# Norm, residual add and transposes between attention and FFN emitted tile by tile instead of phase by phase

## Chip, cores and metric

The kernel runs on all 8 cores of one Trainium2 chip, one batch row of 2048 tokens by 1024 features on each, with no traffic between the cores. The metric is the device time of the slowest core in microseconds (us).

## What is computed

```
x = x + layernorm(attn(layernorm(x)))
x = x + layernorm(ffn(layernorm(x)))
attn(x):  proj = layernorm(x) @ W_in -> v, g0, g1
          y = conv128(v, k0) * g0;  y = conv128(y, k1) * g1      (along the tokens)
          return x + y @ W_out
ffn(x):   s = sigmoid(x @ enc_W);  cont = s @ s2c_W;  top-2 of 8 experts on cont
          d = sigmoid(sigmoid(moe @ c2s_W) @ dec_W);  return layernorm(d)
```

All of it is float32; the experts use pairs of bf16.

## The kernel before

Each core walks through its 2048 tokens in four chunks of 512 (`q` = 0 to 3). A chunk is four tiles of 128 tokens (`t` = 0 to 3), kept in SBUF side by side as 128 partitions by 4 x 1024 columns: `s_x` (the residual stream), `s_z`, `s_xn`, `s_v`. `s_at` holds the activations transposed, features on the partitions; the matmuls read it.

The program is a list of steps. `S.add(engine, fn, reads, writes)` appends a step to the list of one engine, and a step waits by semaphore for the last writers and readers of the buffers that it names. Nothing reorders: each engine runs its steps in the order in which they were added. So the order of the Python loops is the order of the work on every engine, and a step that waits holds up all that was added behind it on the same engine.

In one chunk the stages are: the input projection (L667), two convolutions through a Fourier transform (L711, L721), the transposes of their result and the output projection (L733 to L772), the stretch that the change touches (L774 to L787), the encoder (L791, first matmul L801, weights through the two halves of `s_wb` by SyncE's DMAs), the experts, the decoder (L1046) and the final norms, which also prepare the next chunk (L1107).

The stretch of the change, with one tile at each step:

- `ln3`: `ln_steps` (L468) normalises `s_xn` tile t into `s_z` tile t. It is a chain between two engines: VectorE takes the statistics (L472, L473) and aggregates them (L475), ScalarE takes the root (L478) and negates the mean (L481), VectorE the reciprocal (L484), ScalarE makes the bias (L487) and applies scale and bias to the tile (L490, 128x1024).
- `res1` (L776): GpSimd adds `s_z` to `s_x`.
- `ln4`: `ln_steps` again, from `s_x` tile t into `s_z` tile t; it needs the sum of `res1`.
- `xfT`: `transpose_tile_to_at` (L540) transposes the eight 128x128 blocks of a tile on TensorE (L544) through the PSUM banks 4 to 7, and ScalarE copies each into `s_at` (L559). With four banks the fifth transpose waits for the first copy.

The loops are by phase. The first loop (L774) goes over the four tiles with ln3 and res1, the second (L785) over the four with ln4, and then `transpose_to_at` (L563) calls `transpose_tile_to_at` for the four tiles:

```
774        for t in range(NTQ):
775            ln_steps(xtile(s_xn, t), xtile(s_z, t), [Bxn[t]], [Bz[t]], "q%d_ln3_%d" % (q, t), slot=t)
776            S.add("gpsimd", lambda v, t=t: v.tensor_tensor(
...
785        for t in range(NTQ):
786            ln_steps(xtile(s_x, t), xtile(s_z, t), [Bx[t]], [Bz[t]], "q%d_ln4_%d" % (q, t), slot=t)
787        transpose_to_at(s_z, lambda tt: [Bz[tt]], "q%d_xfT" % q)
```

The encoder's first matmul reads block 0 of all four tiles, so it comes behind the last transposes on TensorE. The end of the chunk (L1107 to L1120) is already emitted tile by tile and has the same pattern of a norm, eight transposes and eight ScalarE evictions (L553, with scale and bias) for each tile.

Of the kernel before, what the change touches and what calls it, by code (L numbers as in the profile page):

```python
# [16 lines left out]
NTQ = TQ // CH  # L17
# [177 lines left out]
def _build(T, until="full"):  # L195
# [34 lines left out]
    def sb(name, p, cols, dt=F32):  # L230
        return nc.alloc_sbuf_tensor(name, [p, cols], dt).ap()

    s_x = sb("s_x", 128, 4096)
    s_z = sb("s_z", 128, 4096)
# [54 lines left out]
    Bx = [Buf("x%d" % t) for t in range(NTQ)]  # L289
    Bz = [Buf("z%d" % t) for t in range(NTQ)]  # L290
# [38 lines left out]
    def xtile(buf_ap, t):  # L329
        return buf_ap[:, t * D:(t + 1) * D]  # L330
# [137 lines left out]
    def ln_steps(src_ap, dst_ap, rb, wb_, tag, slot=0, extra_reads=()):  # L468
        o = slot * 16
        Bs = Bst[slot]  # L470
        st1 = S.add("vector", lambda v: (
            v.bn_stats(s_st[:, o:o + 6], src_ap[:, 0:512]),  # L472
            v.bn_stats(s_st[:, o + 6:o + 12], src_ap[:, 512:1024]))[-1],  # L473
            reads=[*rb, *extra_reads], writes=[Bs], tag=tag + "_stats")
        st2 = S.add("vector", lambda v: v.bn_aggr(s_st[:, o + 12:o + 14], s_st[:, o:o + 12]),  # L475
                    reads=[Bs], writes=[Bs], tag=tag + "_aggr")
        st3 = S.add("scalar", lambda sc: (
            sc.activation(s_st[:, o + 14:o + 15], s_st[:, o + 13:o + 14],  # L478
                          Act.Sqrt, bias=EPS),
            sc.drain(),  # L480
            sc.activation(s_st[:, o + 9:o + 10], s_st[:, o + 12:o + 13],  # L481
                          Act.Identity, bias=Z0, scale=CM1))[-1],
            reads=[Bs, Bsetup], writes=[Bs], tag=tag + "_sqrt")
        st4 = S.add("vector", lambda v: v.reciprocal(s_st[:, o + 15:o + 16], s_st[:, o + 14:o + 15]),  # L484
                    reads=[Bs], writes=[Bs], tag=tag + "_recip")
        st5 = S.add("scalar", lambda sc: (
            sc.activation(s_st[:, o + 8:o + 9], s_st[:, o + 15:o + 16],  # L487
                          Act.Identity, bias=Z0, scale=s_st[:, o + 9:o + 10]),
            sc.drain(),
            sc.activation(dst_ap, src_ap, Act.Identity,  # L490
                          bias=s_st[:, o + 8:o + 9], scale=s_st[:, o + 15:o + 16]))[-1],
            reads=[Bs, Bsetup, *rb], writes=[*wb_, Bs], tag=tag + "_apply")
        return st5
# [46 lines left out]
    def transpose_tile_to_at(tt, src_buf_ap, rbufs, tag, scale_col=None, bias_col=None):  # L540
        if True:
            for kc in range(8):
                bank = 4 + kc % 4
                S.add("tensor", lambda t, kc=kc, bank=bank, tt=tt: t.transpose(  # L544
                    pb[bank][:, tt * 128:(tt + 1) * 128],
                    src_buf_ap[:, tt * D + kc * 128: tt * D + (kc + 1) * 128],
                    IDENT),
                    reads=[*rbufs, Bsetup], writes=[Bp[bank]],
                    tag=tag + "_tp%d_%d" % (kc, tt))
                dst = s_at[:, kc * 512 + tt * 128: kc * 512 + (tt + 1) * 128]  # L550
                psl = pb[bank][:, tt * 128:(tt + 1) * 128]
                if scale_col is not None:
                    S.add("scalar", lambda sc, kc=kc, dst=dst, psl=psl: sc.activation(  # L553
                        dst, psl, Act.Identity,
                        bias=bias_col[:, kc:kc + 1], scale=scale_col[:, kc:kc + 1]),
                        reads=[Bp[bank], Bsetup], writes=[Bat[kc][tt]],
                        tag=tag + "_ev%d_%d" % (kc, tt))
                else:
                    S.add("scalar", lambda sc, dst=dst, psl=psl: sc.copy(dst, psl),  # L559
                          reads=[Bp[bank]], writes=[Bat[kc][tt]],  # L560
                          tag=tag + "_ev%d_%d" % (kc, tt))

    def transpose_to_at(src_buf_ap, rbufs_of_tile, tag, scale_col=None, bias_col=None):  # L563
        for tt in range(NTQ):
            transpose_tile_to_at(tt, src_buf_ap, rbufs_of_tile(tt), tag,
                                 scale_col=scale_col, bias_col=bias_col)
# [77 lines left out]
    for q in range(NQ):  # L644
# [22 lines left out]
        for ms in range(24):  # L667
            slot = ms % 2
# [65 lines left out]
        for ms in range(8):  # L734
            slot = ms % 2
# [38 lines left out]
        for t in range(NTQ):  # L774
            ln_steps(xtile(s_xn, t), xtile(s_z, t), [Bxn[t]], [Bz[t]], "q%d_ln3_%d" % (q, t), slot=t)
            S.add("gpsimd", lambda v, t=t: v.tensor_tensor(  # L776
                xtile(s_x, t), xtile(s_x, t), xtile(s_z, t), Alu.add),
                reads=[Bx[t], Bz[t]], writes=[Bx[t]], tag="q%d_res1_%d" % (q, t))

        if until == "attn":  # L780
            for t in range(NTQ):
                dma("sync", dy[r0 + t * 128:r0 + (t + 1) * 128, :], xtile(s_x, t),
                    reads=[Bx[t]], chan="x%d" % t, tag="q%d_xout%d" % (q, t))
            continue
        for t in range(NTQ):  # L785
            ln_steps(xtile(s_x, t), xtile(s_z, t), [Bx[t]], [Bz[t]], "q%d_ln4_%d" % (q, t), slot=t)
        transpose_to_at(s_z, lambda tt: [Bz[tt]], "q%d_xfT" % q)  # L787

        of_init = S.add("vector", lambda v: v.memset(s_of[:, :], 0.0),
                        writes=[Bof], tag="q%d_ofinit" % q)  # L790
        for g in range(4):  # L791
            for kc in range(8):
                slot = kc % 2
# [242 lines left out]
        for g2 in range(2):  # L1036
            for kc in range(16):
                slot = kc % 2
# [128 lines left out]
def build_nc(T, until="full"):  # L1167
    nc0, S0 = _build(T, until)
    with nc0.Block() as blk0:
        S0.emit(nc0, blk0, count_mode=True)  # L1170
    counts = _dma_instr_counts(nc0, S0)
    nc, S = _build(T, until)
    weights = {}
    for st0, st in zip(S0.steps, S.steps):
        if st.is_dma and st0.i in counts:
            weights[st.i] = counts[st0.i]
    with nc.Block() as blk:
        S.emit(nc, blk, dma_weights=weights)
    return nc
# [18 lines left out]
```

How the kernel before makes its waits and increments, by code:

```python
            def run(eng):  # L112
# [13 lines left out]
                            if st.chan_before > waited.get(key, 0):  # L126
                                waits[key] = max(waits.get(key, 0), st.chan_before)
                        else:
                            key = ("D", d.chan) if d.is_dma else (d.engine, False)
                            if d.target > waited.get(key, 0):
                                waits[key] = max(waits.get(key, 0), d.target)
                    if need_drain and engine_name in ("vector", "scalar", "gpsimd"):
                        eng.drain()
                        drained_upto = nloc - 1
                    for key, tgt in waits.items():
                        eng.wait_ge(sems[key], tgt)
                        waited[key] = tgt
                    inst = st.fn(eng)
                    if st.inc:
                        assert inst is not None, "step %s needs inc but returned None" % st.tag
                        inst.then_inc(sems[skey(st)], 16 if st.is_dma else 1)
                    if count_mode and st.is_dma:
                        eng.nop()
                    local_idx[id(st)] = nloc
```

## Time and profile before

| | |
|---|---|
| three runs | 3986.25, 4130.44 (median), 4306.42 us |
| profiled execution | 3991.32 us, its span 3989.7 us (core 0, the slowest of 3972.5 to 3989.7) |
| TensorE matmul | 3224.6 us busy (81%) |
| VectorE, ScalarE, GpSimd | 909.3 (23%), 796.4 (20%), 301.6 us (8%) |
| DMA | 203.79 MB, mean 51 GB/s |
| mean granted TensorE clock | 0.903 of 2.4 GHz |

A share of busy time is an average over stages. What this change is worth is read in the four stretches between the last eviction of the output projection and the first encoder matmul. A row of a timeline gives the start, the duration, the engine, the line, what is written and read, how many instructions were merged and, in brackets, how long the engine had been idle and what ended that.

### The profile page before, as it was taken

The numbers are of one execution on the slowest core, as the hardware profiler recorded it, in microseconds if no ns is written. First come the engines' busy times: TensorE is split into PE (matmuls) and PEld (weight loads), VectorE is DVE, ScalarE is ACT, GpSimd is POOL, SyncE is SP. The second block draws the span as 40 slices with busy tenths as digits, with TensorE's granted clock in tenths as the row PEclk, the third lists the DMA queues.
The fourth block names the chain that finished last, engine by engine and source line by source line (L and its number), as shares of the span: only waits on it lengthen the run. The fifth ranks groups of instructions, "written<-read, shape, count | busy, mean of one in ns | idle before, by whom it ended". The sixth has DMA issues, their size and how long they took to land.

```text
span 3989.7 us, 39388 instructions; the slowest of 8 cores (3972.5 to 3989.7 us)
## 1 busy us (share of the span) xinstructions
PE 3224.6 (81%) x14240; PEld 1862.2 (47%) x14240; DVE 909.3 (23%) x1576; ACT 796.4 (20%) x1537; POOL 301.6 (8%) x255
## 2 busy tenths in 40 slices
PE   0698997879769987978939999797975999797893
PEld 0596463323359536322419846432335953632241
DVE  0102531051110452023020153105101045202401
ACT  0300002162230002045050000216223000213502
POOL 1141000000020000000030000000002000000002
PEclk9898998998879998998969999899887999899896
DMA  3252011221123001121212200122122310112121
GB/s 63 52 136 66 0 31 43 64 53 40 66 69 84 24 0 42 61 60 32 71 64 80 66 0 25 44 70 53 37 69 64 83 30 0 42 55 60 38 64 39
DMA packets 241244, 203.79 MB, mean 51 GB/s; under 512 B 45496, under 2 KB 192968, under 8 KB 241056
## 3 DMA queue, kind: packets, MB, share of 16 engines
q1 hardware_dynamic: 231552, 174.10, 15.3%
q0 software_dynamic: 9504, 27.18, 2.8%
q8 instruction: 118, 1.93, 0.2%
q14 instruction: 70, 0.57, 0.0%
HBM read 186.02 MB, written 14.68 MB: 50 GB/s over the span
## 4 chain that ended last, share of the span: by engine, by line
PE 69%; ACT 10%; DMA 6%; DVE 5%; issue 4%; ACTq 3%; POOL 1%; POOLq 1%; DVEq 1%; SPq 0%
PE pb L683 14%; PE pb L1046 11%; PE pb L801 10%; PE pb L750 6%; PE pb L590 3%; PE pb L589 3%; PE pb L592 3%; PE pb L591 3%; PE pb L1026 3%; DMA s_big<-L_ffn_We 2%; DVE s_hl L899 2%; PE pb L625 2%; PE pb L816 2%; PE pb L544 2%; PE pb L626 2%
## 5 line engine op out<-in xcount | busy, mean ns | idle before, releaser
L683 PE MATMUL pb<-s_wb,s_at 128*128 128x128 f32 x6144 | 697.3, 277 | 60.1 <-DMA s_wb<-L_attn_W_in 34.3
L683 PEld LDWEIGHTS pb<-s_wb,s_at 128*128 128x128 f32 x6144 | 696.5, 194 | 61.2 <-issue 61.2
L1046 PE MATMUL pb<-s_big,s_wb 128*128 128x512 f32 x1024 | 451.5, 602 | 18.0 <-ACT s_xn L1056 12.2
L801 PE MATMUL pb<-s_at,s_wb 128*128 128x512 f32 x1024 | 452.7, 598 | 7.1 <-DMA s_wb<-L_ffn_enc_W 6.3
L1046 PEld LDWEIGHTS pb<-s_big,s_wb 128*128 128x128 f32 x1024 | 196.4, 193 | 276.0 <-issue 275.7
L559 ACT COPY s_at<-pb 128x128 f32<-128x128 f32 x256 | 52.4, 270 | 1321.5 <-PE pb L544 1320.0
L801 PEld LDWEIGHTS pb<-s_at,s_wb 128*128 128x128 f32 x1024 | 187.1, 190 | 269.3 <-issue 269.0
L750 PE MATMUL pb<-s_wb,s_at 128*128 128x128 f32 x2048 | 229.6, 275 | 0.0
L750 PEld LDWEIGHTS pb<-s_wb,s_at 128*128 128x128 f32 x2048 | 229.0, 192 | 0.6 <-issue 0.5
L899 DVE TENSOR_TENSOR s_hl<-s_wtmp,s_hh 128x512 bf16<-128x512 f32 x256 | 176.8, 692 | 224.5 <-ACT s_hh L896 186.7
L893 ACT ACTIVATE s_wtmp<-pb,s_be 128x512 f32<-128x512 f32 x256 | 175.7, 686 | 134.5 <-PE pb L884 112.1
L544 PE MATMUL pb<-s_cons,s_xn 128*128 128x128 f32 x128 | 42.0, 438 | 165.1 <-ACT s_xn L535 149.8
L896 ACT CAST s_hh<-s_wtmp 128x512 bf16<-128x512 f32 x256 | 158.6, 619 | 17.0 <-issue 1.0
L776 POOL TENSOR_TENSOR s_x<-s_x,s_z 128x1024 f32<-128x1024 f32 x16 | 37.5, 2346 | 1579.0 <-ACT s_z L490 1579.0
L909 PE MATMUL pb<-s_hh,s_we2h 128*64 128x512 bf16 x256 | 103.7, 405 | 64.1 <-ACT s_hh L896 58.4
L1087 DVE COPY s_z<-pb 128x128 f32<-128x128 f32 x64 | 14.1, 282 | 618.8 <-PE pb L1076 599.9
L704 DVE TENSOR_TENSOR s_big<-pb,s_bias 128x512 f32<-128x512 f32 x64 | 44.2, 691 | 441.0 <-PE pb L683 402.4
L827 DVE CAST s_conth<-s_cont 64x512 bf16<-64x512 f32 x4 | 1.7, 418 | 578.7 <-ACT s_cont L822 578.7
L917 PE MATMUL pb<-s_hl,s_we2h 128*64 128x512 bf16 x256 | 101.0, 395 | 40.1 <-DVE s_hl L899 39.8
L1026 PE MATMUL pb<-s_of,s_wb 64*128 64x512 f32 x128 | 111.9, 1065 | 10.5 <-DVE s_of L945 8.5
L625 PE MATMUL pb<-s_wtmp,s_cons 128*128 128x512 f32 x128 | 73.8, 661 | 52.7 <-DVE s_wtmp L620 52.6
L811 ACT ACTIVATE s_big<-pb,s_encb 128x512 f32<-128x512 f32 x64 | 38.8, 690 | 376.2 <-PE pb L801 376.2
(193 smaller groups left out, 3152.4 us busy)
## 6 DMA issues: line engine op xcount, KB each, us to landing
s_wb<-L_attn_W_in SPq DMA_DIRECT2D x96, 512.0 KB, 3.9
s_wb<-L_ffn_enc_W SPq DMA_DIRECT2D x128, 256.0 KB, 3.1
s_wb<-L_ffn_dec_W SPq DMA_DIRECT2D x128, 256.0 KB, 2.6
s_wb<-L_attn_W_out SPq DMA_DIRECT2D x32, 512.0 KB, 4.2
s_we1h<-we1hd SPq DMA_DIRECT2D x32, 256.0 KB, 2.7
s_we1l<-we1ld POOLq DMA_DIRECT2D x32, 256.0 KB, 3.0
y<-s_x SPq DMA_DIRECT2D x16, 512.0 KB, 2.7
s_bias<-L_attn_b_in SPq DMA_DIRECT2D x96, 64.0 KB, 4.1
```

The source lines that it names most:

```text
L544: S.add("tensor", lambda t, kc=kc, bank=bank, tt=tt: t.transpose(pb[bank][:, tt * 128:(tt + 1) * 128], src_buf_ap[:, tt * D + kc * 128: tt ...
L589: last = t.matmul(pb[bank][:, :], FWD_HI(s_i, 0), prevh, start=True, stop=False)
L590: last = t.matmul(pb[bank][:, :], FWD_HI(s_i, 1), curh, start=False, stop=False)
L625: t.matmul(pb[binv][:, :], G_HI(0), w0, start=True, stop=False)
L683: last = t.matmul(pb[bank][:, tt * 128:(tt + 1) * 128], s_at[:, kc * 512 + tt * 128: kc * 512 + (tt + 1) * 128], wap[:, kc * 128:(kc + 1) ...
L750: last = t.matmul(pb[bank][:, tt * 128:(tt + 1) * 128], s_at[:, kc * 512 + tt * 128: kc * 512 + (tt + 1) * 128], wap[:, kc * 128:(kc + 1) ...
L801: last = t.matmul(pb[mi][:, :], eap[:, mi * 128:(mi + 1) * 128], s_at[:, kc * 512:(kc + 1) * 512], start=(kc == 0), stop=(kc == 7))
L893: sc.activation(t32, pb[bank][:, :], Act.Relu, bias=s_be1[:, e * 8 + mc:e * 8 + mc + 1])
L896: return sc.copy(s_hh[:, hb * 512:(hb + 1) * 512], t32)
L899: S.add("vector", lambda v, hb=hb, t32=t32: v.tensor_tensor(s_hl[:, hb * 512:(hb + 1) * 512], t32, s_hh[:, hb * 512:(hb + 1) * 512], Alu.s ...
L1026: S.add("tensor", lambda t, mc=mc, bank=bank, half=half: t.matmul(pb[bank][:, :], s_wb[0:64, half * 1024 + (mc % 8) * 128: half * 1024 + ( ...
L1046: last = t.matmul(pb[mi][:, :], dap[:, mi * 128:(mi + 1) * 128], s_big[:, kc * 512:(kc + 1) * 512], start=(kc == 0), stop=(kc == 15))
```

## The change

The second norm and the transposes move into the loop over the tiles. Tile t now goes through ln3, res1, ln4 and its eight transposes before tile t+1 begins. The steps and their number stay as they are; `until` is "full" here.

```diff
@@ -776,15 +776,16 @@
             S.add("gpsimd", lambda v, t=t: v.tensor_tensor(
                 xtile(s_x, t), xtile(s_x, t), xtile(s_z, t), Alu.add),
                 reads=[Bx[t], Bz[t]], writes=[Bx[t]], tag="q%d_res1_%d" % (q, t))
+            if until != "attn":
+                ln_steps(xtile(s_x, t), xtile(s_z, t), [Bx[t]], [Bz[t]],
+                         "q%d_ln4_%d" % (q, t), slot=t)
+                transpose_tile_to_at(t, s_z, [Bz[t]], "q%d_xfT" % q)
...
-        for t in range(NTQ):
-            ln_steps(xtile(s_x, t), xtile(s_z, t), [Bx[t]], [Bz[t]], "q%d_ln4_%d" % (q, t), slot=t)
-        transpose_to_at(s_z, lambda tt: [Bz[tt]], "q%d_xfT" % q)
```

ScalarE, chunk 0, before: from the last instruction of ln3 of tile 0 over ln3 of tile 1, and then the end of ln4 of tile 3 and the copies (`sem_vector` is a wait for VectorE, `sem_tensor` one for TensorE, `sem_gpsimd` one for GpSimd).

```order
L490 ACTIVATE s_z<-s_xn,s_st 128x1024
L478 ACTIVATE s_st<-s_st 128x1 [waits sem_vector_False]
L481 ACTIVATE s_st<-s_st 128x1
L487 ACTIVATE s_st<-s_st 128x1 [waits sem_vector_False]
L490 ACTIVATE s_z<-s_xn,s_st 128x1024
...
L490 ACTIVATE s_z<-s_x,s_st 128x1024
L559 COPY s_at<-pb 128x128 [waits sem_tensor_False] x32
```

The next norm behind tile 0's ln3 is ln3 of tile 1, and all 32 copies stand in one piece behind the eight norms.

ScalarE, chunk 0, in the changed kernel, from the same instruction on.

```order
L490 ACTIVATE s_z<-s_xn,s_st 128x1024
L478 ACTIVATE s_st<-s_st 128x1 [waits sem_vector_False]
L481 ACTIVATE s_st<-s_st 128x1
L487 ACTIVATE s_st<-s_st 128x1 [waits sem_vector_False,sem_gpsimd_False]
L490 ACTIVATE s_z<-s_x,s_st 128x1024
L559 COPY s_at<-pb 128x128 [waits sem_tensor_False] x8
L478 ACTIVATE s_st<-s_st 128x1 [waits sem_vector_False]
```

Behind the norm of `s_xn` (ln3, tile 0) there now stands the norm of `s_x` (ln4) of the same tile, then its eight copies, and only then ln3 of tile 1.

VectorE, chunk 0, before: ln3 of tile 0 and what follows it.

```order
L472 BN_STATS s_st<-s_xn 128x6
L473 BN_STATS s_st<-s_xn 128x6
L475 BN_AGGR s_st<-s_st 128x2
L484 RECIPROCAL s_st<-s_st 128x1 [waits sem_scalar_False]
L472 BN_STATS s_st<-s_xn 128x6
```

Tile 1's statistics of `s_xn` follow without a wait.

VectorE, chunk 0, in the changed kernel, from the aggregation of ln3 of tile 0 on.

```order
L475 BN_AGGR s_st<-s_st 128x2
L484 RECIPROCAL s_st<-s_st 128x1 [waits sem_scalar_False]
L472 BN_STATS s_st<-s_x 128x6 [waits sem_gpsimd_False,sem_scalar_False]
L473 BN_STATS s_st<-s_x 128x6
L475 BN_AGGR s_st<-s_st 128x2
L484 RECIPROCAL s_st<-s_st 128x1 [waits sem_scalar_False]
L472 BN_STATS s_st<-s_xn 128x6
```

The statistics of `s_x`, which wait for GpSimd's addition, moved in front of the statistics of `s_xn` of tile 1, and those stand behind the whole ln4 of tile 0.

## Rows read from the trace of the kernel before

**Rows 1.** The page, part 4: the chain that ended last, by engine.

```profile
PE 69%; ACT 10%; DMA 6%; DVE 5%; issue 4%; ACTq 3%; POOL 1%; POOLq 1%; DVEq 1%; SPq 0%
```

**Rows 2.** Windows, chunk 0: us, busy of PE, PEld, DVE, ACT, POOL, clock, DMA, GB/s.

```profile
612.00:628.00 16.00, 0.00 (x0) 0.00 (x0) 9.69 (x24) 11.30 (x21) 9.38 (x4) 0.53 0.04 15
628.00:636.00 8.00, 1.09 (x4) 0.72 (x4) 3.84 (x10) 6.34 (x12) 0.00 (x0) 0.50 0.00 1
636.00:643.00 7.00, 6.45 (x29) 4.86 (x30) 0.00 (x0) 6.68 (x33) 0.00 (x0) 0.70 0.01 2
```

**Rows 3.** Timeline, chunk 0: ln3 and res1 of tile 0.

```profile
612.43 0.69 DVE L472 BATCH_NORM_STATS2 s_st<-s_xn 128x6 f32<-128x512 f32 x1
614.11 0.30 ACT L478 ACTIVATE s_st<-s_st 128x1 f32<-128x1 f32 x1 [60.39 <-DVE s_st L475]
615.68 1.24 ACT L490 ACTIVATE s_z<-s_xn,s_st 128x1024 f32<-128x1024 f32 x1
616.83 0.28 ACT L478 ACTIVATE s_st<-s_st 128x1 f32<-128x1 f32 x1
617.13 2.34 POOL L776 TENSOR_TENSOR s_x<-s_x,s_z 128x1024 f32<-128x1024 f32 x1 [285.20 <-ACT s_z L490]
```

**Rows 4.** Timeline, chunk 0: ln4, transposes, copies and the first encoder matmuls.

```profile
626.57 1.24 ACT L490 ACTIVATE s_z<-s_x,s_st 128x1024 f32<-128x1024 f32 x1
628.07 1.09 PE L544 MATMUL pb<-s_cons,s_z 128*128 128x128 f32 x4 [17.36 <-ACT s_z L490]
630.64 0.28 ACT L478 ACTIVATE s_st<-s_st 128x1 f32<-128x1 f32 x1
632.25 1.24 ACT L490 ACTIVATE s_z<-s_x,s_st 128x1024 f32<-128x1024 f32 x1
636.16 0.75 ACT L559 COPY s_at<-pb 128x128 f32<-128x128 f32 x4
636.55 6.32 PE L544 MATMUL pb<-s_cons,s_z 128*128 128x128 f32 x28 [7.39 <-ACT s_at L559]
637.08 6.14 ACT L559 COPY s_at<-pb 128x128 f32<-128x128 f32 x28 [0.18 <-PE pb L544]
642.70 2.80 PE L801 MATMUL pb<-s_at,s_wb 128*128 128x512 f32 x6
```

**Rows 5.** Timeline, chunk 3: first statistics of ln3, first encoder matmuls.

```profile
3468.94 0.69 DVE L472 BATCH_NORM_STATS2 s_st<-s_xn 128x6 f32<-128x512 f32 x1
3499.68 7.09 PE L801 MATMUL pb<-s_at,s_wb 128*128 128x512 f32 x16
```

**Rows 6.** Timeline, end of chunk 0, where the work already goes tile by tile.

```profile
1087.95 2.65 PE L544 MATMUL pb<-s_cons,s_xn 128*128 128x128 f32 x8 [12.43 <-ACT s_xn L535]
1088.50 2.92 ACT L553 ACTIVATE s_at<-pb,s_bA,s_gA 128x128 f32<-128x128 f32 x8 [0.69 <-PE pb L544]
1091.27 0.33 ACT L478 ACTIVATE s_st<-s_st 128x1 f32<-128x1 f32 x1
...
1099.52 2.34 POOL L1115 TENSOR_TENSOR s_v<-s_v,s_gb 128x1024 f32<-128x1024 f32 x1 [0.15 <-issue]
1101.97 0.69 DVE L472 BATCH_NORM_STATS2 s_st<-s_v 128x6 f32<-128x512 f32 x1 [3.45 <-POOL s_v L1115]
```

**Rows 7.** Windows of TensorE alone, chunk 0: us, busy us, clock, DMA share, GB/s.

```profile
636.50:639.50 3.00, 2.95 (x13) 0.50 0.00 0
639.50:640.50 1.00, 1.00 (x6) 0.67 0.00 0
640.50:642.50 2.00, 2.00 (x11) 1.00 0.03 8
```

**Rows 8.** Timeline: the first decoder matmuls of chunk 0.

```profile
946.39 14.01 PE L1046 MATMUL pb<-s_big,s_wb 128*128 128x512 f32 x27 [0.93 <-ACT s_big L1031]
```

**Rows 9.** Timeline of ScalarE, chunk 0: the copies ahead of ln3, and a table load.

```profile
547.49 6.24 ACT L559 COPY s_at<-pb 128x128 f32<-128x128 f32 x31 [0.87 <-PE pb L544]
...
671.50 1.28 ACT L811 ACT_TABLE_LOAD   x1 [28.27 <-PE pb L801]
```

## The prediction

> **What bounds the kernel now.** I read the chain that ended last first. TensorE carries 69% of it [rows 1], so any stretch in which TensorE stands still is paid in full. Then I cut chunk 0 into windows around the edited loops [rows 2]. From 612 to 628 TensorE does nothing, from 628 to 636 it has 1.09 us of work, and from 636 to 643 it runs the transposes. In the same 31 us ScalarE is busy 11.30 + 6.34 + 6.68 = 24.3 us, more than any other engine. So the stretch is bounded by ScalarE with its short chains to VectorE, and its length goes one for one into the time.
>
> The length before: from the first statistics of ln3 to the first encoder matmul it is 642.70 - 612.43 = 30.27 us in chunk 0 [rows 3, 4] and 3499.68 - 3468.94 = 30.74 us in chunk 3 [rows 5]. I take 30.5 us for each of the four chunks, 122 us in all, 3% of the time.
>
> Why it is as short as that: ln3 of tile 0 takes its root at 614.11, and ln3 of tile 1 at 616.83 [rows 3]. So eight norms pass at some 2.7 us each, since the statistics of the next tile and GpSimd's addition (617.13 to 619.47) lie beside ScalarE's work on another tile. The transposes come last, where the copies set the pace: 28 in 6.14 us [rows 4], 0.22 us each.
>
> **The change, part by part.** No instruction is added or removed, and no DMA. What moves is the order on three engines, and with it three things lose their cover.
>
> 1. The addition. VectorE now has ln4's statistics of tile t directly behind ln3's reciprocal, and they wait for GpSimd. ScalarE has ln4's root next, so it stands as well. Queued behind this wait on VectorE are ln3's statistics of tile t+1, on ScalarE the whole of ln3 of tile t+1, and TensorE waits for both. The whole 2.34 us now stands on the path, four times in a chunk.
> 2. The statistics of ln4, which follow the addition: uncovered too. Those of ln3 for tile t+1 stay covered, by ScalarE's apply and copies of tile t.
> 3. The copies. Before, the four transposes that PSUM has room for were ready when the copies began. Now each tile waits for its first transpose, and ScalarE can't start the next norm until the eighth copy.
>
> One tile in the new order, from ln3's root to the root of the next tile's ln3:
>
> - root to end of apply, ln3: 616.92 - 614.11 = 2.81 us [rows 3];
> - to GpSimd's start: 617.13 - 616.92 = 0.21 us, and its addition: 2.34 us [rows 3];
> - to VectorE's start behind GpSimd: 1101.97 - 1101.86 = 0.11 us [rows 6], where VectorE really waits for GpSimd;
> - statistics to root: 614.11 - 612.43 = 1.68 us [rows 3];
> - root to end of apply, ln4: 633.49 - 630.64 = 2.85 us [rows 4];
> - to the first transpose: 628.07 - 627.81 = 0.26 us [rows 4];
> - first transpose to first copy: 1088.50 - 1087.95 = 0.55 us [rows 6], then seven more copies at 0.22 us and 0.27 us for the last: 2.34 us together;
> - the next root overlaps the end of the last copy: -0.10 us (-0.15 in rows 6).
>
> The sum is 12.50 us a tile. A chunk is then 1.68 us for the first statistics, four tiles, 0.10 us given back at the end, less 0.52 us because the encoder starts before the last copy ends (643.22 against 642.70 [rows 4]): 1.68 + 50.00 + 0.10 - 0.52 = 51.3 us. Against 30.5 us that is 20.8 us more in a chunk, 83 us in four.
>
> The copies are the one term that the trace doesn't show in this form. From below: when transposes are ready, four copies take 0.75 us [rows 4], 0.16 us apart, which gives 1.9 us for the piece instead of 2.34. From above: the evictions of the tile-by-tile stage take 2.92 us for eight [rows 6], 3.5 us with the first transpose, but they carry a scale and a bias. I take 0.22 us, because those 28 rows are this same copy, bound by the same four banks.
>
> 4. The clock. Before, the encoder starts behind 28 transposes, at clock 1.00. The clock is 0.50 from 636.5 to 639.5, 0.67 in the next microsecond and 1.00 from 640.5 on [rows 7], and the encoder starts at 642.70. Now only eight transposes, some 1.8 us, stand between a wait of 10 us and the encoder, so its first matmuls run at 1.2 GHz. A start that is cold from the first matmul shows what it costs: the decoder's first 27 matmuls take 14.01 us [rows 8], against 0.59 + 26 x 0.44 = 12.0 us at the encoder's pace at full clock (six in 2.80 us [rows 4]). So 2.0 us is the most that I put for a chunk. If the clock comes back as long behind the first transpose as it did before (some 3.5 us), 1.7 us of the encoder pass at half pace, which loses 0.9 us. The low end is 0.4 us. I take 1.0 us, 4 us in all.
>
> The Trainium skill bears on this term. Its page "TensorE: Matmul & The Clock Gate", section "Part 4: PE-mode transpose", says that transposes don't count as work that lifts the clock. This trace disagrees: from 636.5 to 642.5 TensorE ran nothing but transposes, and the clock rose from 0.50 to 1.00 [rows 7]. By the page the encoder would start wholly cold and pay the 2.0 us, 4 us more over the run; by the row it pays about 1.
>
> Total: 83 + 4 = 87 us. The profiled execution took 3991.3 us, so the forecast is 4078 us, +2.2%. That is made against this execution. It stands at the low end of the three runs shown (3986 to 4306, median 4130), and the ratio, 1.022, is what I would carry to another level. About 2% (80 us) is what a measurement of this kernel can tell from no change.
>
> **What else could move.** The encoder's weights: two slots are filled during the stretch before and after, so their transfers stay covered. Later stages see nothing but a shift.
>
> **Rivals.**
>
> A. The same mechanism, but smaller, ending within 2%. With copies 0.16 us apart and 0.4 us for the clock, a tile is 12.07 us and a chunk 49.5 us: 4 x (19.0 + 0.4) = 78 us, 4069 us, +1.9%. For it: four copies did run at that spacing. Against it: there the transposes had been waiting for 8 us; here each copy is released by a transpose at half clock, and the fifth by a bank.
>
> B. The work hides itself after all, and the time is not slower. ScalarE would have to fill GpSimd's and VectorE's time with another tile. The place is the wait of ln4's root. If all of it were covered, a tile would cost two norms of 2.72 us and eight copies of 0.22 us, 7.2 us, and a chunk some 30 us: 3990 us, no change. The point from which it decides is 7.3 us a tile: above that the new order loses. What speaks for it is that the tail of uncovered copies shrinks from 7 us to 2.3. Against it stands that ScalarE and VectorE both run in program order, and that in the tile-by-tile stage VectorE's statistics sat idle 3.45 us behind GpSimd [rows 6].
>
> C. Something more on the path. If ScalarE had to load a table between copies and root, at 16 places and 1.28 us each, which is what the load ahead of the encoder's sigmoid takes [rows 9], it would be 20 us more, 4098 us. Or the copies go at the pace of rows 6, 1.1 us more a tile, 18 us in all, and the clock costs 2.0 us a chunk: 4100 us. Against the load: copies ended at 553.73 [rows 9] and the root at 614.11 started on VectorE's release [rows 3], with nothing in between.
>
> **How the numbers follow.** The forecast has 0.65; it ends above 2% by a small margin. A has 0.20, B 0.05 and C 0.10. The bounds of the unknown costs are 4069 and 4100; executions of one kernel differ by a few tenths of a per cent, some 12 us, which gives 4055 to 4112. Faster by over 2%: only if B went beyond full cover, 0.01. Within 2%: A and B, 0.24. Slower by over 2%: the forecast and C, 0.75.
>
> **What would show it.** In the changed trace the roots of ln3 of two neighbouring tiles stand 12.5 us apart. VectorE's statistics of `s_x` show some 4.5 us of idle time ahead of them, released by GpSimd, 16 times. TensorE's transposes come as four groups of eight with some 10 us between them. The first encoder matmul comes 51 us behind the first statistics, and the granted clock is 0.50 there, with 1.00 one to two microseconds later. The rest of each chunk keeps its length. It would be wrong if neighbouring roots were under 11 us apart (copies or addition covered), or if the encoder or a later stage changed its length by more than a microsecond or two.

## The result and the profile after

The changed kernel takes 4083.32 us in the median of ten runs, the kernel before 4001.91 us. The ratio is 1.0218, with a 95% interval of 1.0199 to 1.0237. The forecast was 4078 us and a ratio of 1.022. Some executions are slowed by a lower granted clock on one half of the chip or both (the profiled ones of the changed kernel and of e9 on cores 4 to 7), so every ratio is one of the others alone, and all rows of the changed kernel are from core 3. This ratio is that of the means 4082.2 and 3995.1 us. The span of core 3 is 4067.0 us, against 3978.5 us before: 88.5 us more.

The forecast was made against an execution of 3991 us, at the low end of the three runs that were shown then. Their median, 4130 us, isn't the level to set 4078 us against (it would make a gain of the loss that was forecast): seven more runs brought it to 4002.

The timeline of the changed kernel, core 3, chunk 0, from the first statistics of ln3 to the root of tile 1's ln3. It answers to [rows 3], and the brackets are the idle time before an instruction and what ended it:

```profile
611.38 0.69 DVE L472 BATCH_NORM_STATS2 s_st<-s_xn 128x6 f32<-128x512 f32 x1
613.07 0.29 ACT L478 ACTIVATE s_st<-s_st 128x1 f32<-128x1 f32 x1 [60.39 <-DVE s_st L475]
614.63 1.24 ACT L490 ACTIVATE s_z<-s_xn,s_st 128x1024 f32<-128x1024 f32 x1
616.08 2.33 POOL L776 TENSOR_TENSOR s_x<-s_x,s_z 128x1024 f32<-128x1024 f32 x1 [286.51 <-ACT s_z L490]
618.59 0.69 DVE L472 BATCH_NORM_STATS2 s_st<-s_x 128x6 f32<-128x512 f32 x1 [4.51 <-POOL s_x L776]
620.27 0.29 ACT L478 ACTIVATE s_st<-s_st 128x1 f32<-128x1 f32 x1 [4.40 <-DVE s_st L475]
621.89 1.24 ACT L490 ACTIVATE s_z<-s_x,s_st 128x1024 f32<-128x1024 f32 x1
623.41 2.04 PE L544 MATMUL pb<-s_cons,s_z 128*128 128x128 f32 x8 [13.75 <-ACT s_z L490]
623.95 1.86 ACT L559 COPY s_at<-pb 128x128 f32<-128x128 f32 x8 [0.82 <-PE pb L544]
625.70 0.30 ACT L478 ACTIVATE s_st<-s_st 128x1 f32<-128x1 f32 x1
```

One reads the new path down the column: GpSimd's addition ends at 618.41, and VectorE, idle for 4.51 us, starts at 618.59. ScalarE ends its apply at 615.87 and then stands for 4.40 us. In these 4.40 us no compute engine ran anything but the addition and, behind it, the statistics of `s_x` with their aggregation. From root to root a tile takes 625.70 - 613.07 = 12.63 us.

The last tile of the chunk and the encoder, same core; it answers to [rows 4]:

```profile
660.09 1.24 ACT L490 ACTIVATE s_z<-s_x,s_st 128x1024 f32<-128x1024 f32 x1
661.47 2.04 PE L544 MATMUL pb<-s_cons,s_z 128*128 128x128 f32 x8 [10.75 <-ACT s_z L490]
662.01 1.85 ACT L559 COPY s_at<-pb 128x128 f32<-128x128 f32 x8 [0.68 <-PE pb L544]
663.30 29.30 PE L802 MATMUL pb<-s_at,s_wb 128*128 128x512 f32 x64
```

The stretch is 663.30 - 611.38 = 51.92 us. The encoder's first 64 instructions take 29.30 us. (Each float32 matmul of the code shows as two instructions; 64 of them are the encoder's first group of 32.) The same instructions before, on core 3:

```profile
641.74 27.69 PE L801 MATMUL pb<-s_at,s_wb 128*128 128x512 f32 x64
```

And the clock at the encoder's start, in windows of the changed kernel, core 3 (width; busy time of TensorE, its weight loads, VectorE, ScalarE and GpSimd with instruction counts; granted clock; DMA share; GB/s):

```profile
661.00:662.00 1.00, 0.53 (x3) 0.56 (x4) 0.00 (x0) 0.33 (x1) 0.00 (x0) 0.50 0.00 0
662.00:663.00 1.00, 1.00 (x6) 0.70 (x4) 0.00 (x0) 0.95 (x5) 0.00 (x0) 0.50 0.00 0
663.00:664.00 1.00, 1.00 (x4) 0.63 (x3) 0.00 (x0) 0.86 (x4) 0.00 (x0) 0.50 0.00 0
664.00:665.00 1.00, 1.00 (x2) 0.34 (x1) 0.00 (x0) 0.00 (x0) 0.00 (x0) 0.50 0.00 0
665.00:666.00 1.00, 1.00 (x3) 0.46 (x2) 0.00 (x0) 0.00 (x0) 0.00 (x0) 0.50 0.00 0
666.00:667.00 1.00, 1.00 (x3) 0.41 (x2) 0.00 (x0) 0.00 (x0) 0.00 (x0) 0.68 0.00 0
667.00:668.00 1.00, 1.00 (x4) 0.40 (x3) 0.00 (x0) 0.00 (x0) 0.00 (x0) 1.00 0.00 0
```

```profile
663.30:666.60 3.30, 3.30 (x5) 0.50 0.00 0
1638.67:1642.80 4.13, 4.13 (x6) 0.50 0.00 0
2608.83:2612.20 3.37, 3.37 (x5) 0.50 0.00 0
3580.82:3584.90 4.08, 4.08 (x6) 0.50 0.00 0
```

All four chunks of core 3, as differences of such start times ("encoder" is from its first matmul to the table load of its first sigmoid):

| us | stretch, chunks 0 to 3 | sum | encoder, sum |
|---|---|---|---|
| before | 30.24, 30.31, 30.34, 30.61 | 121.5 | 111.3 |
| after | 51.92, 51.13, 51.71, 51.33 | 206.1 | 119.2 |
| difference | | +84.6 | +7.9 |

The rest of core 3's span is 4.0 us shorter. That says nothing of the change: within the profiled execution of the kernel before, the same rest differs by 15 us from core to core (3737.7 to 3752.5 us).

### The profile page after: what moved, and what is told of

The parts are those of the page before. It is cut to its first block, busy times and chain, and to the rows that moved or that the text cites. A ratio compares the mean times of both kernels' runs of the same rounds, so it can differ in the third digit from the quotient of the medians.

```text
span 4183.6 us, 39380 instructions; the slowest of 8 cores (4059.8 to 4183.6 us)
## 1 busy us (share of the span) xinstructions
PE 3348.2 (80%) x14240; PEld 1919.5 (46%) x14240; DVE 910.9 (22%) x1576; ACT 798.0 (19%) x1537; POOL 301.4 (7%) x255
## 4 chain that ended last, share of the span: by engine, by line
PE 70%; ACT 10%; DMA 5%; DVE 5%; issue 4%; ACTq 2%; POOL 2%; POOLq 1%; DVEq 1%; SPq 0%
PE pb L683 14%; PE pb L1047 11%; PE pb L802 11%; PE pb L750 6%; PE pb L590 3%; PE pb L589 3%; PE pb L592 3%; PE pb L591 3%; PE pb L1027 3%; DMA s_big<-L_ffn_We 2%; PE pb L625 2%; PE pb L626 2%; PE pb L817 1%; PE pb L627 1%; DVE s_hl L900 1%
## 5 line engine op out<-in xcount | busy, mean ns | idle before, releaser
L683 PE MATMUL pb<-s_wb,s_at 128*128 128x128 f32 x6144 | 699.5, 278 | 63.2 <-DMA s_wb<-L_attn_W_in 37.5
L683 PEld LDWEIGHTS pb<-s_wb,s_at 128*128 128x128 f32 x6144 | 698.3, 195 | 64.6 <-issue 64.6
L1047 PE MATMUL pb<-s_big,s_wb 128*128 128x512 f32 x1024 | 484.5, 638 | 18.9 <-ACT s_xn L1057 12.2
L802 PE MATMUL pb<-s_at,s_wb 128*128 128x512 f32 x1024 | 477.7, 628 | 3.6 <-DMA s_wb<-L_ffn_enc_W 3.4
L1047 PEld LDWEIGHTS pb<-s_big,s_wb 128*128 128x128 f32 x1024 | 207.1, 204 | 299.1 <-issue 298.0
L802 PEld LDWEIGHTS pb<-s_at,s_wb 128*128 128x128 f32 x1024 | 202.5, 201 | 275.6 <-issue 275.0
L750 PE MATMUL pb<-s_wb,s_at 128*128 128x128 f32 x2048 | 240.8, 283 | 0.0
L750 PEld LDWEIGHTS pb<-s_wb,s_at 128*128 128x128 f32 x2048 | 240.1, 200 | 0.5 <-issue 0.3
L544 PE MATMUL pb<-s_cons,s_z 128*128 128x128 f32 x128 | 32.6, 427 | 181.1 <-ACT s_z L490 181.1
```

Source lines behind the costliest of these rows:

```text
L683: last = t.matmul(pb[bank][:, tt * 128:(tt + 1) * 128], s_at[:, kc * 512 + tt * 128: kc * 512 + (tt + 1) * 128], wap[:, kc * 128:(kc + 1) ...
L750: last = t.matmul(pb[bank][:, tt * 128:(tt + 1) * 128], s_at[:, kc * 512 + tt * 128: kc * 512 + (tt + 1) * 128], wap[:, kc * 128:(kc + 1) ...
L802: last = t.matmul(pb[mi][:, :], eap[:, mi * 128:(mi + 1) * 128], s_at[:, kc * 512:(kc + 1) * 512], start=(kc == 0), stop=(kc == 7))
L1047: last = t.matmul(pb[mi][:, :], dap[:, mi * 128:(mi + 1) * 128], s_big[:, kc * 512:(kc + 1) * 512], start=(kc == 0), stop=(kc == 15))
```

## The experiments

The table has the ratio to the kernel before, run beside each, and the two sums of core 3 as above. e1 to e4 shared one set of runs of the kernel before, e5 to e7 another, e8 and e9 a third. The ratios of e5 and e8 rest on two and four runs.

| | what | ratio, 95% interval | stretch | encoder |
|---|---|---|---|---|
| after | the change | 1.0218 (1.0199 to 1.0237) | 206.1 | 119.2 |
| e1 | ln4 in the loop only | 1.0183 (1.0165 to 1.0202) | 193.6 | 111.3 |
| e2 | transposes in a loop only | 1.0054 (1.0038 to 1.0070) | 134.7 | 116.6 |
| e3 | the change, one tile of skew | 1.0067 (1.0048 to 1.0086) | 141.1 | 118.6 |
| e4 | the change, addition on VectorE | 1.0160 (1.0133 to 1.0187) | 184.1 | 116.2 |
| e5 | the change, 14 extra matmuls | 1.0235 (1.0188 to 1.0282) | 214.8 | 111.1 |
| e8 | the change, 10 extra matmuls | 1.0229 (1.0173 to 1.0285) | 204.6 | 111.4 |
| e6 | order before, gathered copies | 0.9986 (0.9976 to 0.9996) | 104.2 | 116.3 |
| e7 | e6, many extra matmuls | 0.9993 (0.9980 to 1.0007) | 114.3 | 112.1 |
| e9 | e6, few extra matmuls | 0.9950 (0.9928 to 0.9972) | 103.2 | 112.1 |

### One half of the change at a time

e1 takes the transposes out of the loop again:

```diff
             if until != "attn":
                 ln_steps(xtile(s_x, t), xtile(s_z, t), [Bx[t]], [Bz[t]],
                          "q%d_ln4_%d" % (q, t), slot=t)
-                transpose_tile_to_at(t, s_z, [Bz[t]], "q%d_xfT" % q)
...
+        transpose_to_at(s_z, lambda tt: [Bz[tt]], "q%d_xfT" % q)
```

> Only half of the change: ln4 stands behind res1 in the loop over the tiles, the 32 transposes stay behind all norms. My theory: the cost is the cover that GpSimd's addition and ln4's statistics lose. A tile is then the 12.63 us of the changed trace less its copies and first transpose, 9.9 us (2.81 + 0.21 + 2.34 + 0.11 + 1.68 + 2.85 - 0.10). Four of them, 1.68 us of statistics and the old tail of copies (7.0 us, less 0.5) give 47.8 us for the stretch against 30.5 us: +17 us a chunk, +69 us in all, and no cost in the encoder, which again starts behind 28 dense transposes. Rival: the cost comes with the transposes and copies between the norms; then this kernel stays within 20 us of the kernel before.

e2 starts from the kernel before and puts only the transposes into the loop of ln4:

```diff
         for t in range(NTQ):
             ln_steps(xtile(s_x, t), xtile(s_z, t), [Bx[t]], [Bz[t]], "q%d_ln4_%d" % (q, t), slot=t)
-        transpose_to_at(s_z, lambda tt: [Bz[tt]], "q%d_xfT" % q)
+            transpose_tile_to_at(t, s_z, [Bz[t]], "q%d_xfT" % q)
```

> Only the other half: all ln3 and res1 first, then for each tile ln4 and its eight transposes with their copies. My theory: the addition keeps its cover, and what is added is that each tile waits for its first transpose and that no copies run while ScalarE waits for nothing: 12.5 us up to ln4's first root, then 2.85 + 0.28 + 0.54 + 1.86 - 0.16 = 5.4 us a tile, 33.6 us for the stretch, +3 us a chunk. The encoder starts behind one group of eight transposes: between 0 and 2 us a chunk at half clock. Together +12 to +20 us. Rival (the transposes between the norms carry the cost): +70 us or more.

Measured, e1 adds 72.1 us to the stretch and nothing to the encoder, 1.0183 in all, where 69 us were expected. e2 adds 13.2 us to the stretch and 5.3 us to the encoder, 1.0054 in all (some 21 us, where 12 to 20 were expected). So the halves give 85.3 and 5.4 us together, and the whole change 84.6 and 7.9: in the stretch they add up, in the encoder not quite, and four fifths of the cost stand in e1, with the addition. The rival that put it on the transposes falls. The timeline of e1, core 3, one tile from ln3's root to the next, with the same wait as in the changed kernel:

```profile
612.06 0.29 ACT L478 ACTIVATE s_st<-s_st 128x1 f32<-128x1 f32 x1 [60.41 <-DVE s_st L475]
615.08 2.33 POOL L776 TENSOR_TENSOR s_x<-s_x,s_z 128x1024 f32<-128x1024 f32 x1 [285.94 <-ACT s_z L490]
617.58 0.69 DVE L472 BATCH_NORM_STATS2 s_st<-s_x 128x6 f32<-128x512 f32 x1 [4.50 <-POOL s_x L776]
619.26 0.29 ACT L478 ACTIVATE s_st<-s_st 128x1 f32<-128x1 f32 x1 [4.39 <-DVE s_st L475]
622.03 0.28 ACT L478 ACTIVATE s_st<-s_st 128x1 f32<-128x1 f32 x1
```

9.97 us a tile, where the sum said 9.90. In e2 the norms wait for no addition, and a tile of ln4 with its transposes takes 5.3 us:

```profile
635.72 0.30 ACT L478 ACTIVATE s_st<-s_st 128x1 f32<-128x1 f32 x1
638.73 2.04 PE L544 MATMUL pb<-s_cons,s_z 128*128 128x128 f32 x8 [3.26 <-ACT s_z L490]
639.27 1.85 ACT L559 COPY s_at<-pb 128x128 f32<-128x128 f32 x8 [0.68 <-PE pb L544]
641.02 0.30 ACT L478 ACTIVATE s_st<-s_st 128x1 f32<-128x1 f32 x1
```

Most of e2's 3.3 us a chunk in the stretch is one wait: ScalarE idles 0.68 us or more in each tile for the first transpose, at least 2.7 us a chunk, where before the first four copies found their transposes ready [rows 4].

### The cover given back by a skew

e3 stays tile by tile, but ln3 of tile t+1 goes ahead of ln4 of tile t:

```diff
             if until != "attn":
-                ln_steps(xtile(s_x, t), xtile(s_z, t), [Bx[t]], [Bz[t]],
-                         "q%d_ln4_%d" % (q, t), slot=t)
-                transpose_tile_to_at(t, s_z, [Bz[t]], "q%d_xfT" % q)
+                for u in ([t - 1] if t else []) + ([t] if t == NTQ - 1 else []):
+                    ln_steps(xtile(s_x, u), xtile(s_z, u), [Bx[u]], [Bz[u]],
+                             "q%d_ln4_%d" % (q, u), slot=u)
+                    transpose_tile_to_at(u, s_z, [Bz[u]], "q%d_xfT" % q)
```

> The changed kernel with one tile of skew: ln3 and res1 of tile t+1 stand ahead of ln4 and the transposes of tile t; the work is still tile by tile. My theory: what costs is only that nothing covers the addition, so the skew gives that back: 1.68 + 4 x 2.75 + 4 x 2.85 + 4 x 2.5 - 0.4 = 33.7 us for the stretch, +3 us a chunk, and 2 us a chunk for the clock in the encoder as in the changed kernel: +20 us against the kernel before, where the change costs 88. Rival (alternating between two norms and copies is what costs, by short waits at every handover): more than half of the 88 us stays.

The ratio is 1.0067: of the change's 2.2% one and a half come back. That leaves some 27 us, where 20 were expected (the two sums give 19.6 and 7.3 us). The stretch is 35.3 us a chunk where 33.7 were expected. The missing 1.6 us stand at one place, in the first tile, where one norm isn't enough to cover the addition (ScalarE idles there 1.2 to 1.6 us in the four chunks). Timeline of e3, core 3:

```profile
617.62 2.34 POOL L776 TENSOR_TENSOR s_x<-s_x,s_z 128x1024 f32<-128x1024 f32 x1 [287.48 <-ACT s_z L490]
620.06 0.69 DVE L472 BATCH_NORM_STATS2 s_st<-s_x 128x6 f32<-128x512 f32 x1 [1.74 <-POOL s_x L776]
621.74 0.29 ACT L478 ACTIVATE s_st<-s_st 128x1 f32<-128x1 f32 x1 [1.64 <-DVE s_st L475]
```

For the later tiles the eight copies of the tile before lie between as well, and ScalarE's wait is gone. So the rival (alternating norms and copies is what costs) falls; what costs is a chain with nothing of another tile in its gaps.

### The addition made shorter

e4 is the changed kernel with `res1` added to VectorE's list:

```diff
-            S.add("gpsimd", lambda v, t=t: v.tensor_tensor(
+            S.add("vector", lambda v, t=t: v.tensor_tensor(
                 xtile(s_x, t), xtile(s_x, t), xtile(s_z, t), Alu.add),
```

> The changed kernel with res1's addition on VectorE instead of GpSimd. My theory: the addition stands on the path 16 times. A 128x1024 addition on VectorE should take about 1.3 us (two 128x512 ones take 0.69 each) and start some 0.1 us behind the apply, against 0.21 + 2.34 + 0.17 us now: 1.2 us less a tile, 19 us less than the changed kernel, +69 us against the kernel before. Rival: the addition lies beside something else that is as long; then nothing changes, +88 us.

The stretch is 22.0 us shorter than in the changed kernel, 1.4 us for each of the 16 tiles; 1.2 were expected. Timeline of e4, core 3:

```profile
610.05 1.24 ACT L490 ACTIVATE s_z<-s_xn,s_st 128x1024 f32<-128x1024 f32 x1
611.39 1.23 DVE L776 TENSOR_TENSOR s_x<-s_x,s_z 128x1024 f32<-128x1024 f32 x1 [1.89 <-ACT s_z L490]
612.71 0.69 DVE L472 BATCH_NORM_STATS2 s_st<-s_x 128x6 f32<-128x512 f32 x1
```

From the end of the apply to the statistics it takes 1.42 us here and 2.72 us in the changed kernel: 1.30 us less, and the stretch is 1.38 us a tile shorter. What was taken off the addition came off the stretch in full, which is what being on the path means, and the rival (it lies beside something as long) falls. The whole time agrees, 1.0160 where 69 us make 1.017. The encoder is 3.0 us shorter too, which wasn't expected: the clock rises 2.2 to 2.7 us behind its start here.

### The clock at the encoder's start

e5 gives TensorE something to do while it waits for the last tile:

```diff
                 transpose_tile_to_at(t, s_z, [Bz[t]], "q%d_xfT" % q)
+                if t == NTQ - 2:
+                    def warm_fn(te):
+                        last = None
+                        for _ in range(14):
+                            last = te.matmul(pb[3][:, :], IDENT, s_cons[:, 0:512],
+                                             start=True, stop=True)
+                        return last
+                    S.add("tensor", warm_fn, reads=[Bsetup], writes=[Bp[3]],
+                          tag="q%d_warm" % q)
```

> The changed kernel with 14 extra 128x512 matmuls on TensorE (into PSUM bank 3, which is free then) between the transposes of tile 2 and those of tile 3, where TensorE waits 10.5 us for the last norms. They compute nothing that is used. My theory: what the change costs in the encoder (its first 64 matmuls take 29.4 to 30.1 us instead of 27.8) is the clock alone, granted at 0.50 for the first 3 us. If the extra matmuls lift it and it falls again only after a while, the encoder runs at full clock: 8 us less in all, and the stretch itself as long as before (51.5 us). If the clock has fallen again by the time the transposes come (they end some 2.5 us before the last transposes start), nothing changes. Rival: the encoder is slower by its DMAs or by PSUM; then 8 us stay while the clock is 1.00.

e5 was mis-sized: 28 instructions for 14 matmuls held the last transposes back by 2.6 us a chunk. But it answered its question: the encoder takes 111.1 us in four chunks, as before the change. e8 has 10 in place of 14.

> The kernel e5 with 10 extra matmuls in place of 14. In e5 each of them ran as two passes, so 28 passes took 13.3 us and held tile 3's transposes back by 2.6 us a chunk, while the encoder's first 64 matmuls were back at 27.8 us. With 20 passes they should end some 0.7 us ahead of the transposes. My theory: the stretch is that of the changed kernel or a little less (51.5 us, the transposes run faster), the encoder's 64 take 27.8 us: 8 us less than the changed kernel, +80 us against the kernel before. Rival: the clock falls in the gap, then +88 us.

In e8 the stretch is 204.6 us and the encoder 111.4 us: 9.3 us less together than in the changed kernel. Core 3 of e8, the timeline of chunk 0 and two windows (columns as above):

```profile
651.94 10.04 PE L787 MATMUL pb<-s_cons 128*128 128x512 f32 x20
662.90 0.63 PE L544 MATMUL pb<-s_cons,s_z 128*128 128x128 f32 x4 [0.92 <-ACT s_z L490]
664.35 27.69 PE L811 MATMUL pb<-s_at,s_wb 128*128 128x512 f32 x64
```

```profile
662.00:664.35 2.35, 1.28 (x9) 1.01 (x9) 0.00 (x0) 1.78 (x7) 0.00 (x0) 1.00 0.00 0
664.35:666.00 1.65, 1.65 (x5) 0.82 (x5) 0.00 (x0) 0.52 (x4) 0.00 (x0) 1.00 0.00 0
```

The clock stays at 1.00 over the gap of 0.92 us, and the encoder's 64 instructions take 27.69 us, to the hundredth what they took before. The rival (DMAs or PSUM) falls. In the whole time the saving isn't seen: the intervals of e5 and e8 are 0.9 and 1.1% wide, and hold the change's own ratio as well as one that is 9 us lower. The claim rests on the stages, not on the ratio.

### A version that beats both

What an order by tile can give is transposes that run under the norms. e6 takes that alone. It starts from the kernel before, puts each tile's transposes behind its ln4, but into eight banks and with no copy; eight copies of 128x512, four on each of two engines, stand behind the last norm:

```diff
         for t in range(NTQ):
             ln_steps(xtile(s_x, t), xtile(s_z, t), [Bx[t]], [Bz[t]], "q%d_ln4_%d" % (q, t), slot=t)
-        transpose_to_at(s_z, lambda tt: [Bz[tt]], "q%d_xfT" % q)
+            for kc in range(8):
+                S.add("tensor", lambda te, kc=kc, t=t: te.transpose(
+                    pb[kc][:, t * 128:(t + 1) * 128],
+                    s_z[:, t * D + kc * 128: t * D + (kc + 1) * 128], IDENT),
+                    reads=[Bz[t], Bsetup], writes=[Bp[kc]],
+                    tag="q%d_xfT_tp%d_%d" % (q, kc, t))
+        for kc in range(8):
+            eng = "scalar" if kc % 2 == 0 else "vector"
+            S.add(eng, lambda e, kc=kc, eng=eng: (
+                e.copy if eng == "scalar" else e.tensor_copy)(
+                s_at[:, kc * 512:(kc + 1) * 512], pb[kc][:, :]),
+                reads=[Bp[kc]], writes=list(Bat[kc]), tag="q%d_xfT_ev%d" % (q, kc))
```

> The order by phase of the kernel before, but the transposes of each tile stand behind its ln4 and write the tile's 128 columns of eight PSUM banks, one bank for each block, with no copy between; behind the last norm eight copies of 128x512 bring the banks to SBUF, four on ScalarE and four on VectorE, in place of 32 copies of 128x128 on ScalarE. My theory of what an order by tile can gain (transposes under the norms) without what it loses (the addition stays covered, nothing is put between two norms on ScalarE): the encoder starts 2.4 us behind the last apply instead of 6.45, the stretch is 26.5 us instead of 30.4, -16 us in all; the encoder pays 1.5 to 2 us a chunk for the clock, since its transposes are no longer dense. Together -8 to -10 us. Rival: the copies and transposes weren't the limit of the tail, then 0, or +6 us with the clock.

Timeline of e6, core 3, chunk 0:

```profile
635.79 1.24 ACT L490 ACTIVATE s_z<-s_x,s_st 128x1024 f32<-128x1024 f32 x1
637.18 1.94 PE L788 MATMUL pb<-s_cons,s_z 128*128 128x128 f32 x8 [0.81 <-ACT s_z L490]
637.72 2.05 ACT L795 COPY s_at<-pb 128x512 f32<-128x512 f32 x4 [0.68 <-PE pb L788]
637.95 2.48 DVE L795 COPY s_at<-pb 128x512 f32<-128x512 f32 x4 [2.76 <-PE pb L788]
639.38 10.88 PE L812 MATMUL pb<-s_at,s_wb 128*128 128x512 f32 x22 [0.26 <-ACT s_at L795]
```

The last apply of the kernel before, core 3, whose encoder starts at 641.74:

```profile
634.01 1.24 ACT L490 ACTIVATE s_z<-s_x,s_st 128x1024 f32<-128x1024 f32 x1
```

The encoder starts 2.35 us behind the last apply, where it was 641.74 - 635.25 = 6.49 us. That is 17.3 us less in four stretches, 16 expected; the encoder gives 5.0 us back. Some 3.8 us of that are its clock, which is 0.50 for the first 1.4 to 2.4 us of each chunk's encoder (7.7 us in all, half of it lost); the rest isn't taken apart. The ratio, 0.9986, is a gain of 6 us (2 to 10 by its interval) where 8 to 10 were expected and the two sums give 12.3, and small against the 2.2% that the change costs.

e7 and e9 add matmuls that nothing reads, to lift the clock ahead of the encoder (`ln3` is the last step of the last ln3); e9 differs from e7 only in their numbers (7 in place of 14 at the start, 2, 3 and 5 in place of 6, 8 and 12 behind the tiles):

```diff
+        def warm_up(n, deps=()):
+            def fn(te):
+                last = None
+                for _ in range(n):
+                    last = te.matmul(pb[7][:, 384:512], IDENT, s_cons[:, 0:128],
+                                     start=True, stop=True)
+                return last
+            S.add("tensor", fn, reads=[Bsetup], writes=[Bp[7]], deps=deps,
+                  tag="q%d_warm" % q)
+        warm_up(7, deps=[ln3])
...
+            if t < NTQ - 1:
+                warm_up((2, 3, 5)[t])
```

> The kernel e6 with extra 128x128 matmuls on TensorE, unused: 14 once the last ln3 is done, then 6, 8 and 12 behind the transposes of tiles 0, 1 and 2, so that TensorE is busy from some 3 us ahead of the first transposes on. My theory: the encoder then starts at clock 1.00 and the 6 to 8 us of e6 go: -16 us against the kernel before. Rival: the extra matmuls delay the last transposes or the clock isn't granted for them; then as e6 or worse.

> The kernel e7 with fewer extra matmuls (7, then 2, 3 and 5, two passes each), since those of e7 held the first transposes back and cost 2.5 us a chunk in the stretch. My theory: a stretch of 26.2 us as in e6 and 28.0 us for the encoder's first 64: 17 us less than the kernel before in the stretch, nothing lost in the encoder, 3971 us where the kernel before takes 3988. Rival: the extra work on TensorE costs elsewhere what it gives in the encoder, then no better than e6 (-6 to -12 us).

e7's extra work stood in the way: its stretch is 10.1 us longer than e6's, and the ratio, 0.9993, can't be told from 1, where 16 us less were expected. In e9 both sums are right, 103.2 and 112.1 us, 17.5 us less than before together, and the ratio is 0.9950 (0.9928 to 0.9972), some 20 us, where 17 were expected. It is the furthest ahead; of the others only e6's interval lies below 1 at all.

## Why the prediction was right or wrong

**The bound and the mechanism** were right. Nothing was added, and the order alone cost 84.6 us in the stretches, by the steps named: VectorE idles 4.4 to 4.8 us ahead of the statistics of `s_x` (forecast "some 4.5"), 16 times, and the roots stand 12.4 to 12.8 us apart.

**The sum for a tile** was 12.50 us and is 12.63. The pieces: root to apply end 2.80 (2.81), to GpSimd 0.21 (0.21), its addition 2.33 (2.34), to VectorE 0.18 (0.11), statistics to root 1.68 (1.68), to apply end 2.86 (2.85), to the first transpose 0.28 (0.26), transposes and copies 2.40 (2.34). (The forecast's own piece for transposes and copies adds up to 2.36, not 2.34, which changes nothing.) 83 us were forecast for four stretches and 84.6 came. The copies, the one term left open between 1.9 and 3.5 us, fell at the value chosen, which was taken from the copies of the same form.

**The clock** is the term that was mis-sized, and it is the step that failed: 1.0 us a chunk was taken, and core 3 shows 2.0 us (7.9 us in all; 1.6 to 2.4 us in single chunks). Over cores 0 to 3 the mean is 1.6 us. The step rested on "if the clock comes back as long behind the first transpose as it did before (some 3.5 us)", which left 1.7 us of the encoder at half pace. In the four chunks of core 3 it came back 5.2, 6.0, 5.2 and 6.1 us behind the first of the eight transposes, so 3.3, 4.2, 3.4 and 4.2 us of the encoder passed at half pace, and half of that is 7.6 of the 7.9 us. The signs named in advance say the same: 1.00 "one to two microseconds later" came 3.3 us later or more, and the encoder grew by 1.6 to 2.4 us a chunk, where "more than a microsecond or two" was to count as wrong. The upper bound of 2.0 us was low as well: it took 0.44 us an instruction, and 64 in 27.69 us are 0.433, which makes the decoder's start [rows 8] 2.2 us dearer than full pace.

The page "TensorE: Matmul & The Clock Gate" of the Trainium skill, section "Part 4: PE-mode transpose", would have had the encoder start wholly cold and pay 2.0 us, and core 3's 2.0 us agree with it, while the mean of 1.6 us lies between it and the forecast. Yet in the kernel before the clock rose with nothing but 28 transposes running [rows 7], so transposes do count here. What sets the place where it rises stays open: four chunks with the same order of work differ by 0.9 us, and no run separates eight transposes from what stood before them. That it is the clock and neither DMAs nor PSUM is shown by e8.

**The rest.** 83 + 4 us were forecast and 88.5 us seen on core 3 (84.6 + 7.9 - 4.0). The two misses, 1.6 and 3.9 us, have one sign, and 4.0 us elsewhere, less than what separates two cores of one execution there, have the other. So it is luck that the whole change came out at the forecast 87 us (4082.2 - 3995.1): the match is closer than the steps earn.

**The rivals.** A (within 2%) needed copies 0.16 us apart; eight take 1.86 us here, 0.23 us apart. The interval of the ratio does reach down to 1.0199, so "over 2%" is likely rather than proven. B (the work hides itself) would have needed 7.3 us a tile. e3 shows what it takes: the cover comes from the order of the steps, not from the engines. C's table load didn't come: the root at 625.70 follows the copies with nothing between. Nor did its slower copies, but its clock term (2.0 us a chunk) is what core 3 showed.

## What to carry to other kernels

On engines that run in program order, a loop by tile with a chain over several engines shows every link of that chain; a loop by phase, or a skew of one tile, puts another tile's work into the gaps. Before moving steps into a loop, write one tile's chain down with its waits and compare it with the pitch that the phases reach (here 12.6 us against two norms of 2.7 and eight copies of 0.22, 7.2 us).
